# Experts in pair blocks and single blocks, value products in two halves

## The chip, the cores and the metric

The kernel runs on one core of one Trainium2 chip. The metric is the device time of one execution in microseconds; lower is better.

## The reference

A macaron layer on x of 4 x 1024 tokens with 128 features: half a mixture of experts, attention, half a mixture again, each on a layer-normed input and added to x.

```python
x = x + 0.5 * ffn(layernorm(x))
x = x + attention(layernorm(x))
x = x + 0.5 * ffn(layernorm(x))

def ffn(x):                       # D = 128, H = 512, E = 8 experts, top 2
    xf = layernorm(x, g, b)
    scores, idx = top_k(xf @ router_w, 2); gate = softmax(scores)
    # sum over the token's two experts of gate * expert(xf)
def expert(x):
    x = layernorm(x, g, b)
    x1 = x @ W1 + b1
    x2 = clip(x @ W2 + b2, -20, 20)
    hidden = clip(x1 * silu(x2), -1e4, 1e4)
    return clip(hidden @ Wo + bo, -1e4, 1e4)

def attention(x):                 # 16 heads of 8 features, q = k = v
    qkv = x @ W_qkv.T             # per head
    return (softmax(q q^T / sqrt(8)) q) @ W_o.T
```

## The kernel before, in words

There are three stages: experts, attention, experts.

**Experts.** Routing scatters every token's normed row twice into a DRAM buffer with one region per expert (`rows_dram`; a row carries its gate and where its result goes). `vector_lay_out` then computes on VectorE, from the counts of the experts, which expert and which rows each block has. A block is 256 rows (`BLOCK`), two tiles of 128, of one expert; there are 39 blocks (`BLOCKS`), enough for any split of 8192 rows over eight experts. The same program serves all counts, so unused blocks are computed too. Behind the last row of every expert stands filler, written by SyncE (`sync_experts`, L649, eight DMAs).

For a block, SyncE loads the expert's record of weights (`sync_load_record`, L687) and the rows (`sync_load_rows`, L692), six blocks ahead. TensorE turns the rows (`tensor_turn`, L1652). `tensor_chunk` (L1689, L1691) makes four chunks of the hidden layer, W2 and W1 side by side in one PSUM bank. Each f32 product is two instructions, each with its weight load, so a block has 16 of these and 8 in the second product (`tensor_second`, L1700). Per chunk VectorE clips (L1432), ScalarE applies silu (L1091) and VectorE combines (L1442). Then VectorE clips the hidden layer (L1449), TensorE makes the second product, ScalarE adds the bias (L1099), VectorE clips (L1455), TensorE turns back (L1710), ScalarE weighs by the gate tile by tile (L1108), and GpSimd scatters each tile (L963). The order on TensorE is written out in `tensor_experts`: chunk 0, turn back of block i - 2, turn of block i + 1, chunks 1 and 2, second product of block i - 1, chunk 3. Every step waits on a semaphore of the step before it.

**Attention.** The 16 heads of 4 batches are 16 teams of four heads. A team has two halves of 512 queries, and a half has 8 units (128 keys each) of four score slots, one a head. TensorE walks the slots two at a time, called a step here: `tensor_scores` (L1772 to L1778) makes two banks of scores of 128 keys by 512 queries, two row groups of the array side by side; `tensor_row_max` (L1753, L1754) makes scores the other way round into two banks, for the row maxima of a later team, which VectorE reduces (L1496, or L1501 where the two banks do not lie together). ScalarE takes the exponential of each slot (L1133). Once in two steps, `tensor_values(n)` (L1793) multiplies the four heads' exponentials of unit n by the values, 16 output columns for each head, the four heads side by side in four column groups: eight instructions of 512 columns. They add up in `value_bank` over the 8 units of a half; then ScalarE copies it (`finish`, L1151) and the half is turned, scaled and projected.

The order is fixed: at slots 4m + 2 the unit m - 1 follows.

```python
                if slot % UNIT and slot > UNIT:
                    tensor_values(slot // UNIT - 1)
```

The seven PSUM banks of attention are a ring (`Ring`, `att_bank`): whoever fills a bank waits until the seventh holder before it has been read, so a step, which takes four banks, waits for readers of the step before it and of the one before that. `tensor_values` waits until the last slot of its unit is read (`emptied(("score", UNIT * (n + 1) - 1))`), and at the first unit of a half for `value_copied`. ScalarE waits before each fourth slot for the unit two before it (`valued`), since there are eight buffers of exponentials. Chores (transposes, projections, the routing of the next stage) are planned slot by slot in `chores`. The last team has no row maxima left to make.

## Time and profile before

| what | value |
|---|---|
| median of 3 runs | 1529.58 us (1526.94 to 1529.65) |
| the profiled execution | 1530.78 us, of which 1529.0 us from its first to its last instruction |
| busy, TensorE / VectorE / ScalarE / GpSimd | 1262.8 / 1173.5 / 886.3 / 518.2 us |
| mean granted TensorE clock | 0.94 |

Times in the rows are microseconds from the start of the span unless marked ns. PE is TensorE's matmul side, PEld its weight loads, DVE VectorE, ACT ScalarE, POOL GpSimd, SPq the DMA issues of SyncE. A matmul row's time includes the end of the pipeline, so neighbours overlap; distances between starts tell the rate. Busy time of an engine is the time in which any of its instructions runs.

### The profile page before, as it was taken

How to read it: one execution, taken by the hardware profiler on the slowest of the kernel's cores; microseconds unless marked ns; L12 is line 12 of the kernel's file. 1: busy time of each engine (PE TensorE's matmuls, PEld its weight loads, DVE VectorE, ACT ScalarE, POOL GpSimd, SP SyncE). 2: the span in 40 equal slices, each digit the busy share in tenths (PEclk: the TensorE clock that was granted, in tenths of full speed). 3: DMA queues.
4: the chain of work that ended last, by engine and by line, in shares of the span. 5: the costliest groups of instructions: out<-in, count | busy, mean ns of one | idle time of the engine just before them, and what ended most of it. 6: DMA issues, size and time to landing. Idle time of an engine off the chain costs nothing.

```text
span 1529.0 us, 25190 instructions
## 1 busy us (share of the span) xinstructions
PE 1262.8 (83%) x7981; PEld 666.2 (44%) x7981; DVE 1173.5 (77%) x2246; ACT 886.3 (58%) x1874; POOL 518.2 (34%) x602
## 2 busy tenths in 40 slices
PE   2912999996269999999999999899998815999992
PEld 2911888885112222222322223222232214888882
DVE  6771888885398888888898888988989354888884
ACT  1201555553117887777778787777777703555551
POOL 2774333334512200133335324351043440333331
PEclk9999999998559999999999999999999857999996
DMA  7124455542220211102111011110100014554544
GB/s 235 37 63 160 148 187 193 191 172 84 62 81 4 81 34 33 31 12 74 33 35 48 13 54 33 33 46 18 33 2 2 29 53 157 188 195 173 188 164 167
DMA packets 66998, 135.59 MB, mean 89 GB/s; under 512 B 13660, under 2 KB 37056, under 8 KB 66580
## 3 DMA queue, kind: packets, MB, share of 16 engines
q1 hardware_dynamic: 57444, 116.45, 22.5%
q0 software_dynamic: 9088, 16.94, 3.4%
q8 instruction: 67, 1.10, 0.3%
q10 hardware_dynamic: 336, 0.59, 0.1%
q14 instruction: 63, 0.52, 0.1%
HBM read 49.21 MB, written 26.92 MB: 50 GB/s over the span
## 4 chain that ended last, share of the span: by engine, by line
PE 62%; DVE 23%; issue 5%; POOL 5%; DMA 2%; ACT 2%; SPq 2%; POOLq 0%; ACTq 0%; DVEq 0%
DVE att_neg_part L1496 13%; PE psum L1793 10%; PE psum L1700 9%; PE psum L1689 9%; PE psum L1691 9%; PE psum L1772 6%; PE psum L1753 5%; PE psum L1776 4%; POOL rows_dram L954 3%; DVE att_neg_part L1501 2%; PE psum L1635 1%; DVE stats L1228 1%; PE psum L1710 1%; PE psum L1652 1%; ACT att_probs L1133 1%
## 5 line engine op out<-in xcount | busy, mean ns | idle before, releaser
L1133 ACT ACTIVATE att_probs<-psum 128x512 f32<-128x512 f32 x1024 | 534.9, 602 | 115.3 <-PE psum L1778 82.8
L1496 DVE TENSOR_REDUCE att_neg_part<-psum 128x2 f32<-128x1024 f32 x439 | 522.3, 1221 | 96.3 <-PE psum L1754 94.8
L1793 PE MATMUL psum<-att_probs,att_values 128*16 128x512 f32 x2048 | 271.8, 603 | 0.6 <-ACT att_o_t L1151 0.3
L963 POOL DMA_INDIRECT y_dram<-ffn_y,ffn_block_rows x156 | 152.9, 980 | 336.1 <-ACT ffn_y L1108 305.0
L1091 ACT ACTIVATE ffn_silu<-ffn_x2c,ffn_rec 128x256 f32<-128x256 f32 x312 | 158.4, 508 | 158.3 <-DVE ffn_x2c L1432 158.3
L1753 PE MATMUL psum<-att_right,att_left 64*128 64x512 bf16 x512 | 198.2, 388 | 52.4 <-issue 21.8
L1432 DVE TENSOR_SCALAR ffn_x2c<-psum,ffn_rec 128x256 f32<-128x256 f32 x312 | 168.4, 540 | 92.4 <-PE psum L1691 87.6
L1775 PE MATMUL psum<-att_right,att_left 64*128 64x512 bf16 x512 | 198.3, 387 | 11.7 <-DVE att_neg_part L1496 8.8
L1772 PE MATMUL psum<-att_right,att_left 64*128 64x512 bf16 x512 | 197.7, 386 | 5.2 <-DVE att_neg_part L1496 3.7
L1754 PE MATMUL psum<-att_right,att_left 64*128 64x512 bf16 x512 | 201.1, 394 | 0.0
L1776 PE MATMUL psum<-att_right,att_left 64*128 64x512 bf16 x512 | 195.4, 382 | 0.0
L1778 PE MATMUL psum<-att_right,att_left 64*128 64x512 bf16 x512 | 194.8, 380 | 0.0
L1689 PE MATMUL psum<-ffn_block_t,ffn_rec 128*128 128x256 f32 x624 | 188.7, 384 | 1.1 <-ACT ffn_block_t L1059 1.1
L1691 PE MATMUL psum<-ffn_block_t,ffn_rec 128*128 128x256 f32 x624 | 187.5, 382 | 0.0
L1442 DVE SCALAR_TENSOR_TENSOR ffn_hidden<-psum,ffn_rec,ffn_silu 128x256 f32<-128x256 f32 x312 | 149.0, 478 | 15.8 <-ACT ffn_silu L1091 15.5
L885 POOL TENSOR_TENSOR att_max_rest<-att_max_rest,att_max_parts 16x128 f32<-16x128 f32 x64 | 27.7, 432 | 380.6 <-ACT att_max_parts L1189 378.0
L1700 PE MATMUL psum<-ffn_hidden,ffn_rec 128*128 128x256 f32 x624 | 150.1, 384 | 4.1 <-DVE ffn_hidden L1449 4.1
L954 POOL DMA_INDIRECT rows_dram<-rows,place_i x128 | 127.1, 993 | 65.9 <-issue 36.8
L1772 PEld LDWEIGHTS psum<-att_right,att_left 64*128 64x128 bf16 x512 | 47.8, 93 | 209.3 <-ACT att_probs L1133 116.8
L1700 PEld LDWEIGHTS psum<-ffn_hidden,ffn_rec 128*128 128x128 f32 x624 | 119.1, 192 | 22.1 <-DVE ffn_hidden L1449 5.8
L1691 PEld LDWEIGHTS psum<-ffn_block_t,ffn_rec 128*128 128x128 f32 x624 | 120.0, 192 | 16.8
L1753 PEld LDWEIGHTS psum<-att_right,att_left 64*128 64x128 bf16 x512 | 48.0, 94 | 175.1 <-issue 89.9
(181 smaller groups left out, 1513.5 us busy)
## 6 DMA issues: line engine op xcount, KB each, us to landing
ffn_rec<-record SPq DMA_DIRECT2D x78, 776.5 KB, 3.7
ffn_block_rows<-rows_dram SPq DMA_DIRECT2D x78, 130.0 KB, 2.1
att_left<-q_parts_dram SPq DMA_DIRECT2D x64, 96.0 KB
att_right<-q_parts_dram SPq DMA_DIRECT2D x120, 48.0 KB
record<-in_L_ffn_W SPq DMA_DIRECT2D x16, 256.0 KB, 6.7
last_y<-y_dram SPq DMA_DIRECT2D x8, 512.0 KB, 7.4
att_right<-q_parts_dram SPq DMA_DIRECT2D x90, 32.0 KB
y_dram<-ffn_y,ffn_block_rows POOLq DMA_INDIRECT x156, 2.5
```

Of the source, the lines that this page charges most:

```text
L1133: S.activation(probs[:, slot % PROBS, :], ring_bank(("score", slot))[:, :], ACT.Exp, scale=SCALE).then_inc(att_bank.by_act, 1)
L1496: last = V.tensor_reduce(out=neg_part[:, h % 2, keys, p::PAIR, t], in_=psum[:, low:high + 1, :], axis=AX.X, op=ALU.max, negate=True)
L1689: TE.matmul(both[:, 0:BLOCK], rec[:, s, W2 + c * P:W2 + (c + 1) * P], block_t[:, m % 2, :], start=True, stop=True)
L1691: TE.matmul(both[:, BLOCK:2 * BLOCK], rec[:, s, W1 + c * P:W1 + (c + 1) * P], block_t[:, m % 2, :], start=True, stop=True).then_inc(chunke ...
L1700: last = TE.matmul(y_bank[n % 2], rec[:, s, WO + c * F:WO + (c + 1) * F], hidden[:, n % 2, c, :], start=(c == 0), stop=(c == HC - 1))
L1753: TE.matmul(bank[low], left[TOP, s, p, q], right[TOP, s, p, k], start=True, stop=True)
L1754: TE.matmul(bank[high], left[BOTTOM, s, PAIR + p, q], right[BOTTOM, s, PAIR + p, k], start=True, stop=True).then_inc(maxed, 1)
L1772: TE.matmul(low, left[TOP, s, p, k], right[TOP, s, p, q], start=True, stop=False)
L1775: TE.matmul(high, left[BOTTOM, s, PAIR + p, k], right[BOTTOM, s, PAIR + p, q], start=True, stop=False)
L1776: TE.matmul(low, left[TOP, s, PAIR + p, k], right[TOP, s, PAIR + p, q], start=False, stop=True).then_inc(att_bank.filled, 1)
L1778: TE.matmul(high, left[BOTTOM, s, p, k], right[BOTTOM, s, p, q], start=False, stop=True).then_inc(att_bank.filled, 1)
L1793: last = TE.matmul(value_bank[head * VS:head * VS + VW, :], values[:, b % 2, kt, team * TEAM + head, :], probs[:, (UNIT * n + j) % PROBS, ...
```

## The change

The experts' rows are cut into tiles of 128. An expert's tiles go in pairs into blocks of two tiles (32 blocks), and those left over into blocks of one tile (8 blocks), 40 blocks in all. The pair blocks come first, the single ones last. `tiles_of` and `rows_of` give the size of a block, and loads, turns, products, clips, activations and scatters work on that many rows (`few`). `vector_lay_out` computes the owner and the first row of both kinds. A region ends with 128 rows of filler where it had 256.

In attention `tensor_values(n, part)` makes one half of the 512 queries; part 0 follows the scores and the row maximum of slot 4m, part 1 those of slot 4m + 2. Part 0 has the waits, part 1 signals `valued`.

```diff
     BLOCK = 2 * P
     BH = BLOCK // P
-    REGION = TOKENS + BLOCK
-    BLOCKS = (TOPK * TOKENS - E) // BLOCK + E
+    REGION = TOKENS + P
+    PAIRS = ((TOPK * TOKENS - E) // P + 1) // 2
+    BLOCKS = PAIRS + E
+    PAIRED, SINGLE = slice(0, PAIRS), slice(PAIRS, BLOCKS)
...
         def y_scatters(n, r):
 
-            return 16 * BH * len(range(r, n, YSETS))
+            return 16 * sum(tiles_of(m) for m in range(r, n, YSETS))
+
+        def tiles_of(n):
+
+            return BH if n % BLOCKS < PAIRS else 1
+
+        def rows_of(n):
+            return tiles_of(n) * P
...
             for e in range(E):
                 at = Q.value_load(end_i[0:1, e:e + 1], min_val=0, max_val=E * REGION)
-                Q.dma_start(rows_dram[k][bass.ds(at, BLOCK), :], filler_dram[:, :]).then_inc(filler_out[k], 16)
+                Q.dma_start(rows_dram[k][bass.ds(at, P), :], filler_dram[0:P, :]).then_inc(filler_out[k], 16)
...
             row = Q.value_load(whose_i[0:1, 1, i:i + 1], min_val=0, max_val=E * REGION)
-            Q.dma_start(block_rows[:, i % SLOTS, :, :], rows_dram[k][bass.ds(row, BLOCK), :]
-                        .rearrange("(p r) c -> p r c", r=BH)).then_inc(block_in[i % SLOTS], 16)
+            Q.dma_start(block_rows[:, i % SLOTS, 0:tiles_of(i), :], rows_dram[k][bass.ds(row, rows_of(i)), :]
+                        .rearrange("(p r) c -> p r c", r=tiles_of(i))).then_inc(block_in[i % SLOTS], 16)
...
-            settle(V.tensor_scalar(tiles_f[:, :], total, float(BLOCK - 1), None, ALU.add))
+
+            settle(V.tensor_scalar(tiles_f[:, :], total, float(P - 1), None, ALU.add))
             settle(V.tensor_copy(tiles_i[:, :], tiles_f[:, :]))
-            settle(V.tensor_scalar(tiles_i[:, :], tiles_i[:, :], BLOCK.bit_length() - 1, None, ALU.logical_shift_right))
-            settle(V.tensor_copy(tiles_f[:, :], tiles_i[:, :]))
-            settle(V.tensor_tensor_scan(tiles_end[:, :], unit[:, :], tiles_f[:, :], 0.0, ALU.mult, ALU.add))
-            settle(V.tensor_tensor(tiles_start[:, :], tiles_end[:, :], tiles_f[:, :], ALU.subtract))
-            shape = [1, BLOCKS, E]
-            blocks = block_f[:, :].unsqueeze(2).to_broadcast(shape)
+            settle(V.tensor_scalar(tiles_i[:, :], tiles_i[:, :], P.bit_length() - 1, None, ALU.logical_shift_right))
+            V.tensor_copy(tiles_f[:, :], tiles_i[:, :])
+            settle(V.tensor_scalar(pairs_i[:, :], tiles_i[:, :], 1, None, ALU.logical_shift_right))
+            settle(V.tensor_copy(pairs_f[:, :], pairs_i[:, :]))
+            started, ended = ends[:, :, 0:E], ends[:, :, 1:E + 1]
+            settle(V.tensor_tensor_scan(ended[:, 0, :], unit[:, :], pairs_f[:, :], 0.0, ALU.mult, ALU.add))
+            settle(V.tensor_scalar(ended[:, 0, :], ended[:, 0, :], float(PAIRS), None, ALU.min))
+            settle(V.tensor_tensor(in_pairs[:, :], ended[:, 0, :], started[:, 0, :], ALU.subtract))
+            V.tensor_scalar(skipped[:, 0, :], started[:, 0, :], 2.0, None, ALU.mult)
+            settle(V.scalar_tensor_tensor(singles[:, :], in_pairs[:, :], -2.0, tiles_f[:, :], ALU.mult, ALU.add))
+            settle(V.tensor_tensor_scan(ended[:, 1, :], unit[:, :], singles[:, :], 0.0, ALU.mult, ALU.add))
+            settle(V.scalar_tensor_tensor(skipped[:, 1, :], in_pairs[:, :], -2.0, started[:, 1, :], ALU.mult, ALU.add))
             V.memset(passed[:, :, 0:1], 1.0)
-            V.tensor_tensor(passed[:, :, 1:E + 1], blocks, tiles_end[:, :].unsqueeze(1).to_broadcast(shape), ALU.is_ge)
-            settle(V.tensor_tensor(within[:, :, :], blocks, tiles_start[:, :].unsqueeze(1).to_broadcast(shape),
-                                   ALU.subtract))
+            for n, some in enumerate((PAIRED, SINGLE)):
+                shape = [1, some.stop - some.start, E]
+                V.tensor_tensor(passed[:, some, 1:E + 1], block_f[:, some].unsqueeze(2).to_broadcast(shape),
+                                ended[:, n, :].unsqueeze(1).to_broadcast(shape), ALU.is_ge)
+                last = V.tensor_tensor(within[:, some, :], tile_f[:, some].unsqueeze(2).to_broadcast(shape),
+                                       skipped[:, n, :].unsqueeze(1).to_broadcast(shape), ALU.subtract)
+            settle(last)
...
             V.wait_ge(combined, HC * (m + 1))
-            V.tensor_scalar(hidden[:, m % 2, :, :], hidden[:, m % 2, :, :], LIMIT, -LIMIT,
+            few = slice(0, rows_of(i))
+            V.tensor_scalar(hidden[:, m % 2, :, few], hidden[:, m % 2, :, few], LIMIT, -LIMIT,
                             ALU.min, ALU.max).then_inc(hidden_ready, 1)
...
             both = chunk_bank[n % 4]
             if n >= 4:
                 TE.wait_ge(combined, n - 3)
-            TE.matmul(both[:, 0:BLOCK], rec[:, s, W2 + c * P:W2 + (c + 1) * P], block_t[:, m % 2, :],
+            few, w1_few = slice(0, rows_of(i)), slice(BLOCK, BLOCK + rows_of(i))
+            TE.matmul(both[:, few], rec[:, s, W2 + c * P:W2 + (c + 1) * P], block_t[:, m % 2, few],
                       start=True, stop=True)
-            TE.matmul(both[:, BLOCK:2 * BLOCK], rec[:, s, W1 + c * P:W1 + (c + 1) * P], block_t[:, m % 2, :],
+            TE.matmul(both[:, w1_few], rec[:, s, W1 + c * P:W1 + (c + 1) * P], block_t[:, m % 2, few],
...
                 for n in max_units(slot + 1):
                     tensor_row_max(n)
-                if slot % UNIT and slot > UNIT:
-                    tensor_values(slot // UNIT - 1)
+                if slot >= UNIT:
+                    tensor_values(slot // UNIT - 1, slot % UNIT // 2)
                 for chore in chores[slot] + chores[slot + 1]:
                     tensor_chore(*chore)
-            tensor_values(NSCORES // UNIT - 1)
+            for part in range(2):
+                tensor_values(NSCORES // UNIT - 1, part)
...
-        def tensor_values(n):
+        def tensor_values(n, part):
+
             i, u = divmod(n, UNITS)
             half, kt = divmod(u, BT)
             b, team = divmod(i, TEAMS)
-            TE.wait_ge(*att_bank.emptied(("prepare", b, 15)))
-            if kt == 0:
-                if 2 * i + half:
-                    TE.wait_ge(value_copied, 2 * i + half)
-                else:
-                    TE.wait_ge(value_bank_blanked, 1)
-            TE.wait_ge(*att_bank.emptied(("score", UNIT * (n + 1) - 1)))
+            if part == 0:
+                TE.wait_ge(*att_bank.emptied(("prepare", b, 15)))
+                if kt == 0:
+                    if 2 * i + half:
+                        TE.wait_ge(value_copied, 2 * i + half)
+                    else:
+                        TE.wait_ge(value_bank_blanked, 1)
+                TE.wait_ge(*att_bank.emptied(("score", UNIT * (n + 1) - 1)))
+            q = slice(part * HALF // 2, (part + 1) * HALF // 2)
             for j, head in enumerate(HEAD_OF):
-                last = TE.matmul(value_bank[head * VS:head * VS + VW, :], values[:, b % 2, kt, team * TEAM + head, :],
-                                 probs[:, (UNIT * n + j) % PROBS, :], start=(kt == 0), stop=(kt == BT - 1))
-            last.then_inc(valued, 1)
+                last = TE.matmul(value_bank[head * VS:head * VS + VW, q], values[:, b % 2, kt, team * TEAM + head, :],
+                                 probs[:, (UNIT * n + j) % PROBS, q],
+                                 start=(kt == 0 and part == 0), stop=(kt == BT - 1 and part == 1))
+            if part == 1:
+                last.then_inc(valued, 1)
```

## Rows read from the trace of the kernel before

**Rows 1.** The page, costliest groups: busy us, mean ns; idle before, releaser.

```profile
L1133 ACT ACTIVATE att_probs<-psum 128x512 f32<-128x512 f32 x1024 | 534.9, 602 | 115.3 <-PE psum L1778 82.8
L1496 DVE TENSOR_REDUCE att_neg_part<-psum 128x2 f32<-128x1024 f32 x439 | 522.3, 1221 | 96.3 <-PE psum L1754 94.8
...
L1091 ACT ACTIVATE ffn_silu<-ffn_x2c,ffn_rec 128x256 f32<-128x256 f32 x312 | 158.4, 508 | 158.3 <-DVE ffn_x2c L1432 158.3
...
L1432 DVE TENSOR_SCALAR ffn_x2c<-psum,ffn_rec 128x256 f32<-128x256 f32 x312 | 168.4, 540 | 92.4 <-PE psum L1691 87.6
...
L1442 DVE SCALAR_TENSOR_TENSOR ffn_hidden<-psum,ffn_rec,ffn_silu 128x256 f32<-128x256 f32 x312 | 149.0, 478 | 15.8 <-ACT ffn_silu L1091 15.5
```

**Rows 2.** Stretches: length, busy PE, PEld, DVE, ACT, POOL, clock, DMA share, GB/s.

```profile
160.01:362.08 202.07, 202.07 (x1008) 177.84 (x1007) 166.83 (x360) 118.34 (x287) 70.77 (x72) 1.00 0.48 174
...
455.71:1176.90 721.19, 685.94 (x5161) 202.59 (x5164) 629.69 (x866) 562.24 (x1124) 212.77 (x289) 1.00 0.12 33
1176.90:1223.01 46.11, 38.38 (x274) 11.06 (x273) 19.16 (x69) 33.36 (x69) 18.92 (x22) 0.89 0.08 25
```

**Rows 3.** Timeline of TensorE over one block of experts: start, duration, line.

```profile
255.37 1.89 PE L1700 MATMUL psum<-ffn_hidden,ffn_rec 128*128 128x256 f32 x8
...
260.99 0.38 PE L1700 MATMUL psum<-ffn_hidden,ffn_rec 128*128 128x256 f32 x1
```

**Rows 4.** Timeline of TensorE over one round of attention.

```profile
803.39 0.39 PE L1772 MATMUL psum<-att_right,att_left 64*128 64x512 bf16 x1
...
803.83 0.38 PE L1753 MATMUL psum<-att_right,att_left 64*128 64x512 bf16 x1
...
804.26 0.38 PE L1776 MATMUL psum<-att_right,att_left 64*128 64x512 bf16 x1
...
804.77 0.37 PE L1753 MATMUL psum<-att_right,att_left 64*128 64x512 bf16 x1
...
805.09 1.05 PE L1793 MATMUL psum<-att_probs,att_values 128*16 128x512 f32 x8
806.07 0.39 PE L1772 MATMUL psum<-att_right,att_left 64*128 64x512 bf16 x1
```

**Rows 5.** Timeline of ScalarE and VectorE in the same round.

```profile
804.02 2.07 ACT L1133 ACTIVATE att_probs<-psum 128x512 f32<-128x512 f32 x4 [0.62 <-PE psum L1778]
...
804.25 2.36 DVE L1496 TENSOR_REDUCE att_neg_part<-psum 128x2 f32<-128x1024 f32 x2 [0.33 <-PE psum L1754]
```

**Rows 6.** Timeline of TensorE, a projection of 128 columns in attention.

```profile
626.15 1.16 PE L1827 MATMUL psum<-wo_t,att_xh_t 128*128 128x128 f32 x8
```

**Rows 7.** Chain that ended last, first stage: the fold, one column wide.

```profile
59.03 3.20 PE psum L1601 x16
```

**Rows 8.** Groups by line, VectorE from SBUF to SBUF: busy us, mean ns.

```profile
L1449 DVE TENSOR_SCALAR ffn_hidden<-ffn_hidden 128x1024 f32<-128x1024 f32 x78 | 54.1, 694 | 2.7
...
L1455 DVE TENSOR_SCALAR ffn_y_t<-ffn_y_t 128x256 f32<-128x256 f32 x78 | 23.3, 299 | 35.3 <-ACT ffn_y_t L1099 35.3
```

**Rows 9.** Timeline of the tail of the first experts' stage.

```profile
367.23 3.18 PE L1700 MATMUL psum<-ffn_hidden,ffn_rec 128*128 128x256 f32 x8 [1.80 <-DVE ffn_hidden L1449]
...
372.02 0.62 ACT L1108 ACTIVATE ffn_y<-psum,ffn_block_rows 128x128 f32<-128x128 f32 x2 [1.11 <-PE psum L1710]
373.42 0.98 POOL L963 DMA_INDIRECT y_dram<-ffn_y,ffn_block_rows  x1 [3.94 <-ACT ffn_y L1108]
374.71 0.98 POOL L963 DMA_INDIRECT y_dram<-ffn_y,ffn_block_rows  x1 [0.30 <-issue]
```

**Rows 10.** Timeline before the second experts' stage: SyncE's fillers, the layout's end.

```profile
1251.28 9.73 SPq L649 DMA_DIRECT2D rows_dram<-filler_dram  x8
...
1254.92 0.39 DVE L1394 CAST whose_i<-whose 1x78 int32<-1x78 f32 x1
```

**Rows 11.** Timeline of ScalarE, the copy of the value bank.

```profile
616.06 0.59 ACT L1151 COPY att_o_t<-psum 128x512 f32<-128x512 f32 x1
```

**Rows 12.** Timeline of TensorE, the last team.

```profile
1188.55 1.05 PE L1793 MATMUL psum<-att_probs,att_values 128*16 128x512 f32 x8
...
1190.50 1.05 PE L1793 MATMUL psum<-att_probs,att_values 128*16 128x512 f32 x8
```

54 lines of the change are left out of this document (35 added, 19 removed).

## Prediction

> **What bounds the kernel now.** I read the page first. Its costliest groups [rows 1] belong to two different stages, the exponentials and row maxima of attention and the clips and products of the experts, on all three engines; so the next view is the table of stretches [rows 2]. In the first experts' stage TensorE is busy for the whole 202.07 us, VectorE for 166.83: TensorE sets the pace, and whatever shortens its work shortens the stage. In attention (721.19 us for 15 of the 16 teams) TensorE is busy 685.94, VectorE 629.69 and ScalarE 562.24, but that busy time includes the overlapping ends of matmuls; only the order of starts tells what is work and what is wait.
>
> The timeline of a block of experts [rows 3] shows the eight second products starting at 255.37 and again at 260.99: 5.62 us for one block. Eight products of 256 columns take 1.89, so (1.89 - 0.38) / 7 = 0.216 each, the last one lasting 0.38; 24 products at 0.216 are 5.18, and the four transposes get the other 0.44, 0.11 each. 36 blocks lie in the 202.07 us, 5.61 each.
>
> The timeline of attention [rows 4] shows one round of four score slots, one unit of value products: scores at 803.39, a row maximum at 803.83, the second scores, whose last products start at 804.26, the row maximum at 804.77, values at 805.09, the next scores at 806.07: 2.68 us. Scores cost 0.44, and a row maximum 0.22. The second row maximum would follow 804.26 by 0.22 and starts 0.29 after that: it needs the bank of the score whose exponential starts at 804.02 [rows 5], lasts 0.60 [rows 1] and is seen by TensorE at 804.77, a release of 0.15. This is the one wait in an ordinary round. VectorE's two maxima take 2.36 of the 2.68 and ScalarE's four exponentials 2.07 [rows 5]. So the round is TensorE's work, 2.39, plus 0.29 of waiting. The 240 units of 15 teams are 643 us at that rate; the other 78 are chores (transposes, projections, routing) and VectorE's busier rounds.
>
> **The change part by part: experts.** Each stage has 39 blocks of two tiles now, 32 of two and 8 of one after: 7 blocks of 5.62 go (39.3 us), 8 small ones come. A small block issues the same 24 products with the same weights on 128 columns, and two transposes. Half of 0.216 would be 0.108. The nearest row for 128 columns and 128x128 f32 weights is the projection of attention [rows 6]: eight in 1.16, or 0.126 each if the last one lasts about as long as a transpose, 0.28. The bound on the other side is the fold of the first stage, one column wide [rows 7]: 16 in 3.20, 0.20 each, where nothing covers the weight load. I take 0.126, since width and weights agree: 24 x 0.126 + 2 x 0.11 + 0.06 = 3.3 us. By 0.20 it would be 5.1, by 0.108 2.9.
>
> The Trainium skill ("TensorE: Matmul & The Clock Gate", LDWEIGHTS) says that a weight load costs its columns divided by 1.2 GHz; for 128 that is an estimate of 107 ns, which would make a small block about 2.9 us. The trace's 0.126 is above it.
>
> VectorE and latency must fit into the 3.3. Durations by width, from SBUF: 694 against 299 ns for 1024 and 256 elements, 0.51 ns each [rows 8]; from PSUM (1221 - 540) / 768 = 0.89 ns each, maxima against clips [rows 1]. So a clip goes from 540 to about 430 ns, a combine from 478 to 365, a silu from 508 to about 400, the clip of hidden from 694 to 430, that of y from 299 to 230. VectorE's ten add up to 3.8; neighbours overlap, as the maxima do by 0.08 (two in 2.36 at 1.22 each), which brings it to 3.1: just inside. Latency is the tighter one: the second product of a block waits for the last clip (0.43), silu (0.40), combine (0.37), clip of hidden (0.43) and four hand-overs, about 1.9 us after the last first product; TensorE has three chunks and two transposes, 1.7, to put there. I add 0.2: 3.5 us a small block, bounds 2.9 and 5.1. Per stage: -39.3 + 28.0 = -11.3.
>
> The small blocks stand last, so the tail behind the last block shortens too. Its eight second products take 3.18 us [rows 9], 0.4 each where a full block has 0.216; by the 0.126 doubled they would be 2.1, and I take 0.9 off. One transpose of two saves 0.2, the vector and scalar steps about 0.8, one weighing of two 0.3 (two take 0.62, [rows 9]), and one scatter of two 1.29, the distance of their issues. That is -3.5 a stage. Both stages: 2 x (-11.3 - 3.5) = -30.
>
> **The layout** of blocks gets some eight more VectorE instructions of 0.16 to 0.2 us. In the second stage they run under the eight fillers of SyncE, which take 9.73 us [rows 10], and the layout before ends 1255.31, 5.7 before those do; cost nothing, 1.5 without that cover. The fillers move half as many bytes: between 0 and -2, I take -1.
>
> **Attention.** A unit's eight value products of 512 columns become twice eight of 256, one half after every row maximum. A unit costs 0.98 from its start to the next scores: two waves of 2 x 0.216, and 0.12 more. And the step into it costs 0.32 after a row maximum, where the next scores would come after 0.22: 0.10 more. These two extras, 0.22, are paid twice per round. A half is 0.43 + 0.12 = 0.55. A step is then 0.22 + 0.22 + 0.32 + 0.55 = 1.31 to 1.32, a round 2.63. Does the wait come back? The row maximum needs the previous step's first exponential, seen at 0.63 + 0.60 + 0.15 = 1.38 after its scores; it now comes at 1.31 + 0.44 = 1.75. The wait of 0.29 is gone. But the first half of a unit now follows the scores of slot 4m and needs the exponential of slot 4m - 1, where before it had a step more. That is seen at 0.63 + 0.49 + 0.60 + 0.15 = 1.87, the values stand at 1.31 + 0.76 = 2.07: 0.2 to spare. VectorE needs 2.36 of 2.63. So 2.68 becomes 2.63, -0.05 a round; rounds in which VectorE sets the pace gain nothing, I count 180 of 240: -9.
>
> The Trainium skill ("TensorEngine Tiling (Array Packing)", Key Properties) says that a change of tiling mode drains the engine. The trace agrees with its 0.10 before and 0.12 behind a unit; the rule speaks against halves.
>
> Two places lose. At the end of each half of a team the value bank is copied (0.59, [rows 11]), and the next unit, which waits for the copy, now starts a step earlier. The copy stands behind two exponentials, starts 0.63 + 2 x 0.49 = 1.61 after the scores and is seen at 2.35, against 2.07: 0.28 x 30 = +8. Behind the copying ScalarE instruction stand the next exponentials, 0.15 late, which is within their slack. And the last team has rounds without row maxima, 1.95 apart [rows 12]. Apart from the unit's 0.98 a round there is 0.44 and 0.22 of scores and 0.31 of step into the unit. A step would be 0.22 + 0.31 + 0.55 = 1.08, with the first half waiting for 1.87 instead of 1.08 + 0.53: 2 x 1.08 + 0.26 = 2.42, +0.47 over 11 rounds: +5. Attention: -9 + 8 + 5 = +4.
>
> **Sum:** -30 - 1 + 4 = -27. The profiled execution took 1530.8 (1529.0 of span, 1.8 around it), 1.2 over the median of 1529.6; a difference carries over unchanged: 1529.6 - 27 = 1502.6, say 1503.
>
> **The rivals.** (A, forecast, 0.62.) Experts give 30, attention about nothing. Own range 1490 to 1515, from small blocks of 2.9 to 4.1 us and 0.05 us either way a round.
>
> (B, 0.10.) Halves are really half: 0.49 instead of 0.55, no extra switches, a step 1.25 and a round 2.50. 0.18 x 240 = 43 instead of 9: 1469. For it speaks that VectorE would still fit (2.36); against it that no value group in the trace is followed by scores in under 0.98.
>
> (C, 0.12.) Small blocks are bound by weight loads at 0.20, or by the latency chain at 5.1 us: a stage changes by 8 x 5.1 - 39.3 = +1.5, less 3.5 of tail, both -4; with -1 and +4 the total is -1: 1529. At 4.3 us it would be 1516. The 0.126 speaks against it.
>
> (D, other side, 0.16.) The first half of a value unit waits for the exponential in most rounds, because ScalarE falls behind by more than the 0.2 it has. With the exponential seen 0.45 later than I reckon, every first half is 0.24 late and a round is 2.87: 0.24 x 240 = +58, 1561. It decides from 0.11 a round upward, where it eats the 27. For it: ScalarE's copies of 0.59 stand in the same queue; against it: it has 0.27 idle a step to catch up.
>
> **The numbers.** Slower comes from most of D (0.11; its mild part lands below). No measurable change is 0.2%, 3 us, on either side: half of C and the edge of D, 0.07. The rest, 0.82, is faster. The range runs from between A and B to C: 1484 to 1530, which leaves B and most of D out.
>
> **What would show it.** Experts: second products of the last 7 blocks 3.3 to 3.7 apart, 5.62 in the others; the stage ends some 14 us sooner. In attention, value groups 1.31 apart with row maxima directly behind score pairs; PE should show short waits for ScalarE's o_t copy; the last team's rounds near 2.4. Wrong would be: small blocks at 5 us, value halves preceded by a ScalarE wait everywhere, or a value half taking 0.49.

## The result and the profile after

The changed kernel takes 1502.11 us (median of 4 runs, 1501.35 to 1503.41), the kernel before 1528.26 beside it (4 runs, 1525.86 to 1529.65): a ratio of 0.9833, 95% interval 0.9817 to 0.9849, or 26.2 us less. The forecast was 1503. The profiled span fell from 1529.0 to 1500.9, by 28.1.

First the page of the changed kernel, the groups that answer to [rows 1]. The exponentials are as many and about as long as before; the 4,096 value products are now 256 wide. The clips and silus of the experts are 320 instead of 312, shorter in the mean.

```profile
L1156 ACT ACTIVATE att_probs<-psum 128x512 f32<-128x512 f32 x1024 | 556.6, 596 | 120.4 <-PE psum L1821 90.5
L1536 DVE TENSOR_REDUCE att_neg_part<-psum 128x2 f32<-128x1024 f32 x439 | 530.0, 1223 | 76.7 <-PE psum L1797 63.3
L1839 PE MATMUL psum<-att_probs,att_values 128*16 128x256 f32 x4096 | 320.9, 385 | 6.8 <-ACT att_o_t L1174 4.2
...
L1113 ACT ACTIVATE ffn_silu<-ffn_x2c,ffn_rec 128x256 f32<-128x256 f32 (+1 forms) x320 | 154.8, 487 | 152.2 <-DVE ffn_x2c L1469 152.2
L1469 DVE TENSOR_SCALAR ffn_x2c<-psum,ffn_rec 128x256 f32<-128x256 f32 (+1 forms) x320 | 163.2, 513 | 90.3 <-PE psum L1732 86.4
```

Then the table of stretches, with the columns of [rows 2]. The marks are the same events in both kernels: from the first to the last group of second products of an experts' stage, and from the first value group of a team to that of another.

```profile
160.25:362.40 202.15, 194.25 (x1035) 172.04 (x1033) 163.85 (x379) 116.66 (x294) 68.80 (x70) 0.99 0.47 176
444.70:1158.30 713.60, 701.08 (x7077) 210.30 (x7076) 641.44 (x862) 578.56 (x1124) 213.05 (x289) 1.00 0.12 34
1158.30:1208.30 50.00, 41.19 (x397) 12.51 (x397) 20.39 (x76) 36.48 (x71) 18.92 (x22) 0.93 0.07 23
1271.90:1475.80 203.90, 198.88 (x1061) 175.60 (x1061) 168.49 (x389) 119.61 (x302) 68.44 (x70) 1.00 0.47 174
```

Laid beside [rows 2] this gives the account of the whole span. Fifteen teams: 721.2 to 713.6, -7.6. The last team: 46.1 to 50.0, +3.9. The first experts' stage, from the first group of second products (154.1 before, 154.5 after) to the last (367.2 and 362.4): 213.1 to 207.9, -5.2; the second 213.1 to 203.9, -9.2. Behind the first stage, up to the first value group, -6.2, of it 1.5 because the first half of a unit comes one step of slots earlier (it starts 5.6 behind attention's first scores, the whole unit of before 7.1); behind the second, to the end, 28.8 to 25.1, -3.7. Between attention and the second stage -0.5, and the first stage begins 0.4 later. The sum is -28.1.

Now TensorE over the experts' blocks of one tile. The first row of each block is its transpose of the input (L1692, where an idle time is shown), then its eight second products (L1742).

```profile
332.71 1.16 PE L1742 MATMUL psum<-ffn_hidden,ffn_rec 128*128 128x128 f32 x8 [0.16 <-DVE ffn_hidden L1488]
...
336.19 1.16 PE L1742 MATMUL psum<-ffn_hidden,ffn_rec 128*128 128x128 f32 x8 [0.19 <-DVE ffn_hidden L1488]
...
340.22 0.33 PE L1692 MATMUL psum<-identity,ffn_block_rows 128*128 128x128 f32 x1 [1.82 <-DMA ffn_rec<-record]
341.28 1.06 PE L1742 MATMUL psum<-ffn_hidden,ffn_rec 128*128 128x128 f32 x8
...
345.87 0.33 PE L1692 MATMUL psum<-identity,ffn_block_rows 128*128 128x128 f32 x1 [2.48 <-DMA ffn_rec<-record]
347.68 1.91 PE L1742 MATMUL psum<-ffn_hidden,ffn_rec 128*128 128x128 f32 x8
```

From 332.71 to 336.19 are 3.48 us: the small block of the forecast, 3.5. The next two are 5.09 and 6.40 apart. TensorE stood still for 1.82 and 2.48 us before their transposes, for the load of the expert's weights. Right behind the second idle time the granted clock fell to half, 1.2 GHz, for 3.4 us from 346.1; the products at 347.68 lie in it and take 1.91 instead of 1.16. The record of weights that the second idle time waits for was issued at 342.17 (first fence) and needs 3.6 us to land. The table of waits of SyncE's queue, from 320 to 364, says why it was issued so late (second fence): before it issues a block's loads (L709) SyncE waits for the scatter of the block six before.

```profile
342.17 0.50 SPq L705 DMA_DIRECT2D ffn_rec<-record  x1
```

```profile
SPq L709 <- DMA y_dram<-ffn_y,ffn_block_rows: 13.8, 5, 5.3
```

The DMA engines were not full meanwhile. In the table of stretches their share from 340 to 343, just before the second idle time, is 0.11 (last but one column):

```profile
340.00:343.00 3.00, 2.78 (x25) 2.78 (x25) 1.75 (x7) 1.62 (x5) 0.65 (x1) 1.00 0.11 22
```

Last, TensorE in attention, one ordinary round and the end of a half team, with row maxima (L1796) and value halves (L1839). Value groups stand 1.31 apart, a round is 2.62. At 560.12 the copy of the value bank holds the first half up by 0.17. The last team, without row maxima, has one such wait for an exponential in each round (second fence), 2.43 long where it was 1.95 [rows 12].

```profile
555.64 0.38 PE L1796 MATMUL psum<-att_right,att_left 64*128 64x512 bf16 x1
...
555.95 0.63 PE L1839 MATMUL psum<-att_probs,att_values 128*16 128x256 f32 x8
556.51 0.39 PE L1815 MATMUL psum<-att_right,att_left 64*128 64x512 bf16 x1
...
557.26 0.62 PE L1839 MATMUL psum<-att_probs,att_values 128*16 128x256 f32 x8
...
558.57 0.62 PE L1839 MATMUL psum<-att_probs,att_values 128*16 128x256 f32 x8
...
560.12 0.62 PE L1839 MATMUL psum<-att_probs,att_values 128*16 128x256 f32 x8 [0.17 <-ACT att_o_t L1174]
```

```profile
1172.28 0.63 PE L1839 MATMUL psum<-att_probs,att_values 128*16 128x256 f32 x8 [0.17 <-ACT att_probs L1156]
...
1173.38 0.62 PE L1839 MATMUL psum<-att_probs,att_values 128*16 128x256 f32 x8
...
1174.71 0.63 PE L1839 MATMUL psum<-att_probs,att_values 128*16 128x256 f32 x8 [0.17 <-ACT att_probs L1156]
```

### The profile page after: what moved, and what is told of

It reads as the page before. It is cut to its first block, busy times and chain, and to the rows that moved or that the text cites. A ratio compares the mean times of both kernels' runs of the same rounds, so it can differ in the third digit from the quotient of the medians.

```text
span 1500.9 us, 29407 instructions
## 1 busy us (share of the span) xinstructions
PE 1252.9 (83%) x10053; PEld 656.3 (44%) x10053; DVE 1173.0 (78%) x2286; ACT 895.3 (60%) x1874; POOL 506.2 (34%) x593
## 3 DMA queue, kind: packets, MB, share of 16 engines
q1 hardware_dynamic: 58020, 116.18, 22.8%
## 4 chain that ended last, share of the span: by engine, by line
PE 46%; DVE 18%; issue 4%; ACT 3%; DMA 2%; SPq 2%; POOL 1%; DVEq 0%; POOLq 0%; ACTq 0%
PE psum L1839 13%; DVE att_neg_part L1536 10%; PE psum L1815 7%; PE psum L1819 5%; PE psum L1796 4%; PE psum L1730 4%; PE psum L1732 4%; PE psum L1742 4%; DVE att_neg_part L1541 1%; ACT att_probs L1156 1%; DVE stats L1253 1%; ACT att_o_t L1174 1%; PE psum L1862 1%; DVE x_sb L1505 1%; PE psum L1890 1%
## 5 line engine op out<-in xcount | busy, mean ns | idle before, releaser
L1156 ACT ACTIVATE att_probs<-psum 128x512 f32<-128x512 f32 x1024 | 556.6, 596 | 120.4 <-PE psum L1821 90.5
L1536 DVE TENSOR_REDUCE att_neg_part<-psum 128x2 f32<-128x1024 f32 x439 | 530.0, 1223 | 76.7 <-PE psum L1797 63.3
L1839 PE MATMUL psum<-att_probs,att_values 128*16 128x256 f32 x4096 | 320.9, 385 | 6.8 <-ACT att_o_t L1174 4.2
L984 POOL DMA_INDIRECT y_dram<-ffn_y,ffn_block_rows x144 | 141.2, 980 | 326.5 <-ACT ffn_y L1131 301.7
L1113 ACT ACTIVATE ffn_silu<-ffn_x2c,ffn_rec 128x256 f32<-128x256 f32 (+1 forms) x320 | 154.8, 487 | 152.2 <-DVE ffn_x2c L1469 152.2
L1469 DVE TENSOR_SCALAR ffn_x2c<-psum,ffn_rec 128x256 f32<-128x256 f32 (+1 forms) x320 | 163.2, 513 | 90.3 <-PE psum L1732 86.4
L1796 PE MATMUL psum<-att_right,att_left 64*128 64x512 bf16 x512 | 198.3, 388 | 33.0 <-issue 21.4
L1730 PE MATMUL psum<-ffn_block_t,ffn_rec 128*128 128x256 f32 (+1 forms) x640 | 181.3, 365 | 1.1 <-ACT ffn_block_t L1080 1.1
L1732 PE MATMUL psum<-ffn_block_t,ffn_rec 128*128 128x256 f32 (+1 forms) x640 | 180.5, 364 | 0.0
L1839 PEld LDWEIGHTS psum<-att_probs,att_values 128*16 128x16 f32 x4096 | 68.0, 94 | 223.5 <-issue 124.7
L1480 DVE SCALAR_TENSOR_TENSOR ffn_hidden<-psum,ffn_rec,ffn_silu 128x256 f32<-128x256 f32 (+1 forms) x320 | 144.5, 451 | 18.4 <-ACT ffn_silu L1113 16.9
L1742 PE MATMUL psum<-ffn_hidden,ffn_rec 128*128 128x256 f32 (+1 forms) x640 | 140.4, 363 | 6.4 <-DVE ffn_hidden L1488 6.4
L1815 PEld LDWEIGHTS psum<-att_right,att_left 64*128 64x128 bf16 x512 | 47.4, 93 | 198.1 <-ACT att_probs L1156 127.2
L1742 PEld LDWEIGHTS psum<-ffn_hidden,ffn_rec 128*128 128x128 f32 x640 | 113.2, 192 | 22.7 <-DVE ffn_hidden L1488 9.5
```

The source lines that it names most:

```text
L1156: S.activation(probs[:, slot % PROBS, :], ring_bank(("score", slot))[:, :], ACT.Exp, scale=SCALE).then_inc(att_bank.by_act, 1)
L1536: last = V.tensor_reduce(out=neg_part[:, h % 2, keys, p::PAIR, t], in_=psum[:, low:high + 1, :], axis=AX.X, op=ALU.max, negate=True)
L1730: TE.matmul(both[:, few], rec[:, s, W2 + c * P:W2 + (c + 1) * P], block_t[:, m % 2, few], start=True, stop=True)
L1732: TE.matmul(both[:, w1_few], rec[:, s, W1 + c * P:W1 + (c + 1) * P], block_t[:, m % 2, few], start=True, stop=True).then_inc(chunked, 1)
L1742: last = TE.matmul(y_bank[n % 2][:, few], rec[:, s, WO + c * F:WO + (c + 1) * F], hidden[:, n % 2, c, few], start=(c == 0), stop=(c == HC ...
L1796: TE.matmul(bank[low], left[TOP, s, p, q], right[TOP, s, p, k], start=True, stop=True)
```

## Experiments

They ran in three groups, each on one chip and against the kernel before on the same chip: e1 to e4 (before 1577.86, 18 runs), e5 to e8 (1582.92, 9 runs), e9 to e12 (1579.12, 9 runs). All kernels are some 50 us longer there than in the result above, so only ratios are compared across groups; e12 looks at those 50 us.

### e1: the experts' part alone

The changed kernel with value products whole, as before.

```diff
-                if slot >= UNIT:
-                    tensor_values(slot // UNIT - 1, slot % UNIT // 2)
+                if slot % UNIT and slot > UNIT:
+                    tensor_values(slot // UNIT - 1)
...
```

> The experts' half of the change alone: 32 pair blocks and 8 single ones, value products whole as before. By the prediction's sum the experts give 30 and the fillers 1: 1497. By the reading of the changed kernel's trace, where the second products of the last blocks are 3.48 us apart but two or three gaps in each stage are 4.2 to 6.4, a stage gives 5 to 9 and its tail 3.7: together 22 to 24 off, 1505. Under 1500 the first holds, over 1503 the second.

Measured: 1558.24, ratio 0.9873 (0.9858 to 0.9888), 20.0 us less (17.7 to 22.4). The gain of the change is in the experts, but it is smaller than the 31 of the forecast's terms for them, and near the 22 to 24 read from the trace.

### e2: the value halves alone

The kernel before with the halves, the same lines the other way round.

> The attention's half of the change alone: 39 blocks of two tiles, value products in two halves after every row maximum. The prediction's sum gives +4 (rounds of 2.63 for 2.68, +0.28 at each copy of the value bank, +0.47 a round in the last team): 1532. The trace of the changed kernel suggests about 8 off in 15 teams and 4 on in the last: 1525. Rival: the halves are worth nothing by themselves and the whole gain is the experts': 1529, rounds of 2.68.

Measured: 1579.71, ratio 1.0008 (0.9999 to 1.0017): +1.3 us. The time is the rival's, but not for its reason: the rounds of the third team are 2.62 and not 2.68, and it is the last team and the stalls (e12) that take the gain back. The sum of e1 and e2 is -18.7 here; the whole change on the next chip (e5) gives -21.

### e3: both halves one behind the other

The kernel before, both halves issued at the place of the whole unit.

```diff
                 if slot % UNIT and slot > UNIT:
-                    tensor_values(slot // UNIT - 1)
+                    for part in range(2):
+                        tensor_values(slot // UNIT - 1, part)
...
```

> The kernel before with both halves of a unit of value products issued one behind the other where the whole unit stood (slots 4m + 2). If the price of a half is its place between products of another shape (0.22 us for each entry and exit), the unit costs 0.98 as before and the time stays at 1529, rounds of 2.68. If halving itself costs (twice as many instructions and weight loads, 0.03 to 0.1 a unit), the rounds get longer by that and 240 of them add 7 to 24 us.

Measured: 1582.01, ratio 1.0029 (1.0018 to 1.0039), +4.5 us. The rounds of the trace are 2.69, those of before, and beside e12 each team without a stall but the first is the same to 0.1 us, some 1 us together. A group of sixteen starts 0.990 ahead of the next scores (median), the whole unit of eight 0.985. So twice as many products of half the width cost next to nothing where no other shape stands between them. What halves cost in the change is the second entry and exit, as the forecast had it. Of the 4.5 us some 2 lie in longer stalls (e12); the rest was not located.

### e4: one more buffer for the blocks' loads

The changed kernel with seven sets of input buffers for blocks instead of six, so that SyncE waits for the scatter of the block seven before.

```diff
-    SLOTS = 6
+    SLOTS = 7
```

> The changed kernel with seven instead of six buffers of records and rows, so that a block's load is issued one block sooner. If the gaps of 4.2 to 6.4 us between single blocks come from loads that are issued too late, behind the scatter of the block six before, they shrink to 3.5 and the time falls by 3 to 8 us: 1496. If they come from the DMA engines being full (a record of 776 KB in 3.5 us is 222 GB/s), they stay or move and the time stays within 2 us, or the seventh record before the second stage costs 1.6 more.

Measured: 1553.53, ratio 0.9849 (0.9835 to 0.9862). TensorE's timeline has small blocks 3.48 to 3.55 apart but for one of 3.9 in each stage, whose turn back waits for VectorE, and the stages take 203.0 and 203.1 instead of 207.9 and 203.9:

```profile
353.02 0.39 PE L1732 MATMUL psum<-ffn_block_t,ffn_rec 128*128 128x128 f32 x2
353.67 1.16 PE L1742 MATMUL psum<-ffn_hidden,ffn_rec 128*128 128x128 f32 x8 [0.27 <-DVE ffn_hidden L1488]
...
357.15 1.16 PE L1742 MATMUL psum<-ffn_hidden,ffn_rec 128*128 128x128 f32 x8 [0.27 <-DVE ffn_hidden L1488]
```

SyncE's waits for scatters have not gone; in the same stretch they have grown from 13.8 to 18.6 us:

```profile
SPq L709 <- DMA y_dram<-ffn_y,ffn_block_rows: 18.6, 5, 5.3
```

But no transpose waits for a load any more. The wait of a queue costs nothing until an engine with work stands behind it, and one more buffer puts it out of reach. DMA engines too slow for a record in 3.48 us, the expectation's other branch, would have kept the gaps: that is out.

The traces of all kernels say it more broadly. Eight stages with six buffers (the result, e1, e5, e6) take 203.9 to 208.1, eight with seven (e4, e8, e9, e10) 202.9 to 203.4. What late loads cost thus varies from one execution to the next, 1 to 5 us a stage. In the time of the whole kernel the gain is 4 us where the halves are absent (e1 against e10, in different groups); with them the intervals of e4 and e5 overlap.

### e5: the changed kernel again

No edit, the partner of e6 on its chip.

> The changed kernel once more, beside the others of this group: it gives the profile and the time on the same chip. 26 us under the kernel before if the chips agree. On the chip of the first group the runs had three stalls of 14 to 16 us in attention that neither first trace has, in teams 7, 11 and 15; if they belong to the chip, they are here or not here in all four kernels; if they belong to a kernel, only in some.

Measured: 1561.95, ratio 0.9863 (0.9848 to 0.9878), against 0.9833 in the result: 21 us less and not 26. The stalls (e12) are in all four kernels of this group.

### e6: whole units where a half has to wait

The changed kernel, both halves together at the later place in the units behind a copy of the value bank and in those behind the last row maximum.

```diff
-                if slot >= UNIT:
-                    tensor_values(slot // UNIT - 1, slot % UNIT // 2)
+                unit = slot // UNIT - 1
+                if slot >= UNIT and (unit % BT == 0 or not max_units(slot + 1)):
+                    if slot % UNIT:
+                        tensor_values(unit, 0)
+                        tensor_values(unit, 1)
+                elif slot >= UNIT:
+                    tensor_values(unit, slot % UNIT // 2)
```

> The changed kernel, but the first unit of each half of a team and the units behind the last row maximum are made whole at slots 4m + 2 as before. If the first half waits for the copy of the value bank and, in the last team, for the exponential, as the prediction has it, the rounds of 2.86 become 2.69 (30 x 0.17 = 5) and those of 2.43 become 1.95 (11 x 0.47 = 5): 10 us under the changed kernel. Rival: the 0.24 is ScalarE's delay and comes back a round later, then 5 or less.

Measured: 1558.93, ratio 0.9853 (0.9833 to 0.9873), which the interval doesn't part from e5. The traces do. The last team has rounds of 1.95 again and takes 62.9 instead of 68.0, each with a stall in it (e12). At the copies nothing came: the group of 16 behind the copy stands a step later, and the next one is nearer by as much.

```profile
517.93 0.62 PE L1844 MATMUL psum<-att_probs,att_values 128*16 128x256 f32 x8
520.35 1.06 PE L1844 MATMUL psum<-att_probs,att_values 128*16 128x256 f32 x16
522.67 0.62 PE L1844 MATMUL psum<-att_probs,att_values 128*16 128x256 f32 x8
```

In units, measured between their first products, the two rounds around the copy are 3.73 and 2.33 here and 2.86 and 3.20 in e5, 6.06 in both, and the second and third teams take 45.1 and 43.9 here and 45.1 and 44.0 there. So the rival was right at the copies: the delay comes back a moment later. That it is ScalarE's queue which would charge it is the likely reason and was not tested alone.

### e7: values ahead of the row maximum

A theory of mine: with whole products, placed before the row maximum, TensorE would fill the time in which it waits for the bank. The kernel before with two lines exchanged:

```diff
-                for n in max_units(slot + 1):
-                    tensor_row_max(n)
                 if slot % UNIT and slot > UNIT:
                     tensor_values(slot // UNIT - 1)
+                for n in max_units(slot + 1):
+                    tensor_row_max(n)
```

> The kernel before with one edit: at slots 4m + 2 the whole unit of value products stands ahead of the row maximum instead of behind it. If a round is 2.39 of TensorE's work and 0.29 of waiting for the exponential before the second row maximum, a whole unit (0.98) covers this wait as halves do, without a second entry and exit: rounds of 2.39 to 2.42, VectorE (2.36) just behind. 0.27 x 150 to 200 rounds: 40 to 54 off. Rival: the second row maximum now comes 0.98 later, VectorE idles meanwhile and the wait moves to it: rounds of 2.6 to 2.7, gain under 15.

Measured: 1660.43, ratio 1.049 (1.0476 to 1.0504), +78 us. Every ordinary round is 3.23 long. The timeline of one round, TensorE (scores L1772 and L1775, row maximum L1753) and VectorE:

```profile
559.51 1.05 PE L1793 MATMUL psum<-att_probs,att_values 128*16 128x512 f32 x8
...
560.50 0.39 PE L1753 MATMUL psum<-att_right,att_left 64*128 64x512 bf16 x1
...
560.93 2.36 DVE L1496 TENSOR_REDUCE att_neg_part<-psum 128x2 f32<-128x1024 f32 x2 [0.88 <-PE psum L1754]
...
562.21 0.39 PE L1775 MATMUL psum<-att_right,att_left 64*128 64x512 bf16 x1 [0.47 <-DVE att_neg_part L1496]
...
562.74 1.05 PE L1793 MATMUL psum<-att_probs,att_values 128*16 128x512 f32 x8
```

The value group delays the row maximum by 0.98, VectorE idles 0.88 for it, its reduction ends later, and the next scores (L1775) wait 0.47 for the bank that it holds; they in turn delay the next value group. TensorE and VectorE each wait once a round. The order that fills TensorE's wait starves VectorE, whose two maxima need 2.36 of the 2.68 us. The theory is wrong; the rival had the mechanism but not its size (rounds of 2.6 to 2.7).

### e8: the same order with the experts' part and seven buffers

> The experts' half of the change, seven buffers, and whole units of value products ahead of the row maximum. If the three effects add up: 20 (experts), 4 to 6 (seventh buffer), 40 to 54 (order): 64 to 80 under the kernel before. If the order is worth under 15, 25 to 41.

Measured: 1635.25, ratio 1.032 (1.0304 to 1.0335), rounds of 3.23 again. It was meant as the best version, and falls with e7; from e7 to e8 the experts' part and the seventh buffer take 25 us off.

### e9: seven buffers, and whole units only behind the last row maximum

The changed kernel with the edit of e4 and that part of e6 that brought something.

```diff
-    SLOTS = 6
+    SLOTS = 7
...
+                if slot >= UNIT and not max_units(slot + 1):
+                    if slot % UNIT:
+                        tensor_values(unit, 0)
+                        tensor_values(unit, 1)
+                elif slot >= UNIT:
+                    tensor_values(unit, slot % UNIT // 2)
```

> The changed kernel with seven buffers, and with whole units of value products behind the last row maximum only (the part of the mended kernel that shortened a stretch: the last team took 5 less, the copies nothing). The changed kernel stood at 0.986 on the slower chip and 0.983 on the first. 5 off for the last team and 4 to 6 for the single blocks: 10 under the changed kernel, a ratio of 0.979 to 0.980 on the slower chip. If the two do not add up, 0.983.

Measured: 1550.19, ratio 0.9824 (0.9809 to 0.9840), the fastest version of the study, by its interval below e1 and e5, while those of e4, e6 and e10 overlap it. The 0.979 to 0.980 was missed: the two terms did not add up, and against e5's ratio it is 6 us and not 10.

### e10: the experts' part with seven buffers

> The experts' half of the change with seven buffers, attention wholly as before. The experts' half alone gave 0.987; 4 to 6 for the seventh buffer: 0.984. It is the version to prefer if the halves are worth nothing; against the kernel of the same group with halves it shows what halves are worth once the last team is spared: by the traces 45 of 48 us come in teams 0 to 14 at 0.5 a team less, 7 off. So it should be 0.5% slower than that one, or the same if the longer stalls of the slower chip eat it.

Measured: 1555.31, ratio 0.9846 (0.9832 to 0.9859), 0.0027 or 4 us below e1's ratio, with intervals that just touch. The two experts' stages take 203.2 and 203.0 in its trace, 207.5 and 205.0 in e1's. Against e9, on the same chip, it isolates the halves where row maxima are: e9's trace has fifteen teams in 745.7 us, e10's in 749.6, -3.9; thirteen teams give -5.3 of it, the two with a stall +1.3. That is less than the 7 expected.

### e11: the clip of hidden cut to a quarter in small blocks

The kernel of e4; in the small blocks the clip leaves out three of the four chunks of hidden.

```diff
-            V.tensor_scalar(hidden[:, m % 2, :, few], hidden[:, m % 2, :, few], LIMIT, -LIMIT,
+            chunks = slice(0, HC) if rows_of(i) == BLOCK else slice(HC - 1, HC)
+            V.tensor_scalar(hidden[:, m % 2, chunks, few], hidden[:, m % 2, chunks, few], LIMIT, -LIMIT,
```

> The changed kernel with seven buffers, whose single blocks clip only the last of the four chunks of the hidden layer (the clip of the other three is left out). If a single block's 3.48 us are TensorE's work plus the wait of the second product for this clip (0.43, would be 0.23), the single blocks come 3.28 to 3.32 apart. If weight loads or VectorE's own load set the 3.48, the distance stays.

Measured once: 1552.07. The small blocks come 3.28 apart instead of 3.48, and the rows of the second products show no idle time any more:

```profile
348.07 1.16 PE L1743 MATMUL psum<-ffn_hidden,ffn_rec 128*128 128x128 f32 x8
...
350.96 0.39 PE L1733 MATMUL psum<-ffn_block_t,ffn_rec 128*128 128x128 f32 x2
351.34 1.16 PE L1743 MATMUL psum<-ffn_hidden,ffn_rec 128*128 128x128 f32 x8
...
354.62 1.16 PE L1743 MATMUL psum<-ffn_hidden,ffn_rec 128*128 128x128 f32 x8
```

It looks as if 3.28 were TensorE's own work in a small block, but it is not, for these rows include the end of the pipeline. The distances of starts tell more: the pairs of first products stand 0.22 to 0.23 apart, and from the last pair, 350.96, to the second products are 0.38, so 0.16 of waiting is left. The table of waits of the weight loads, from 343 to 361, has it:

```profile
PEld psum L1743 <- DVE ffn_hidden L1489: 1.2, 5, 0.3
```

Another 0.06 stands before the turn back. In e4 the last pair starts at 353.02 and the second products at 353.67, 0.65 later: a wait of 0.43, of which the row shows 0.27. Both kernels give the same work, 3.48 - 0.43 and 3.28 - 0.16 - 0.06, or 3.05 to 3.06. What sets the distance is the chain from the last first products of a block through clip, silu, combine and clip of hidden to its second products, since it got shorter by just the 0.2 of the edit. VectorE's own load is not wholly out as a rival, for the edit takes 0.2 off that too. It is busy 9.42 of 10.45 us over three blocks of e4, so it is close behind.

### e12: the kernel before, with a profile on this chip

> The kernel before, for its profile on this chip. If the three stalls of 14 to 16 us belong to the chip and not to an edit, teams 7, 11 and 15 have them here too, each about 15 long, and everything else in the trace agrees with the first one within 1 us a team.

Measured once: 1576.31, span 1574.6. The extra time sits in three places: teams 7 and 11 take 63.5 and 63.8 us (48.0 and 48.1 in the profile of the kernel before above) and the last 58.7 (46.1). In each, GpSimd makes a run of 16 routing scatters. TensorE and the chain that ended last, in one of them:

```profile
818.69 0.55 PE L1776 MATMUL psum<-att_right,att_left 64*128 64x512 bf16 x1
819.02 0.63 PE L1778 MATMUL psum<-att_right,att_left 64*128 64x512 bf16 x1
827.29 0.58 PE L1753 MATMUL psum<-att_right,att_left 64*128 64x512 bf16 x1 [7.63 <-ACT att_probs L1133]
```

```profile
813.48 1.75 another core or an unknown queue
...
817.95 7.14 another core or an unknown queue
825.13 1.43 another core or an unknown queue
```

The kernel before, the experts alone (63.3 and 63.7) and the changed kernel (63.7 and 64.5) all have them, at the same two teams. They belong to the chips or the time of these groups and not to the change. In kernels with the halves they are longer: the last team takes 58.7 to 61.6 with whole units (e12, e1, e10) and 65.4 to 68.0 with halves there (e4, e2, e5), of which the longer rounds explain some 4 to 5. One thing in this trace is not as in the first: the last of the fifteen teams, without a stall in either, takes 50.5 here and 51.7 there. With whole units e1 and e10 have 50.6.

## Why the forecast was right, and which of its terms were not

**Bound and mechanism.** Forecast A came in: experts give nearly all. Attention gives 5 in the result's pair of traces and nothing in e2. B is out, since halves are 1.31 apart and not 1.25. C's 5.1 us a small block is out, by 3.48. D is out: of 240 first halves in fifteen teams 21 waited for the copy, 0.2 at most, and none for an exponential by the table of waits of the matmuls. The weight loads have 138 such waits, but they are hidden: first and second halves both start 0.30 to 0.31 behind the row maximum (555.64 and 555.95 above).

**A small block: the sum right, its two parts not.** 3.48 against 3.5. TensorE's own work was forecast as 3.3 and is 3.05. The second products take 1.16 for eight, as the row chosen [rows 6], 0.124 apart. But the sixteen first products stand only 0.111 apart (a pair every 0.22, e4), where all 24 were priced at 0.126. The wait for the second product was forecast as 0.2 and is 0.43: the chain behind the last first product takes 2.04 and not 1.9 (351.63 to 353.67 in e4), and TensorE has 1.61 of work to put there, not 1.7. That the two errors cancel is luck; the latency chain as the tighter bound, which the forecast named, is confirmed by e11. The durations by width, in the changed kernel's single blocks:

```profile
L1469 DVE TENSOR_SCALAR ffn_x2c<-psum,ffn_rec 128x128 f32<-128x128 f32 x29 | 11.4, 406 | 4.1 <-PE psum L1732 4.1
L1113 ACT ACTIVATE ffn_silu<-ffn_x2c,ffn_rec 128x128 f32<-128x128 f32 x29 | 11.4, 401 | 9.6 <-DVE ffn_x2c L1469 9.6
L1480 DVE SCALAR_TENSOR_TENSOR ffn_hidden<-psum,ffn_rec,ffn_silu 128x128 f32<-128x128 f32 x29 | 10.1, 347 | 2.7 <-ACT ffn_silu L1113 2.1
...
L1488 DVE TENSOR_SCALAR ffn_hidden<-ffn_hidden 128x512 f32<-128x512 f32 x8 | 3.4, 427 | 0.3
```

That is 406, 401, 347 and 427 ns where the forecast had 430, 400, 365 and 430.

**A stage: the term that was mis-sized.** "Per stage: -39.3 + 28.0 = -11.3" measured -5.2 and -9.2; the term was 8.2 us too large over both. It multiplied the small block by eight and asked only whether TensorE, VectorE and the latency fit into it. Two things were left out. The loads have to keep up as well: SyncE's chain of scatter, landing and load goes round once in six blocks, and six small blocks are 21 us where six large ones were 34. That cost 4.9 us in the first stage, the half clock behind the second idle time included, and 0.8 in the second (207.9 and 203.9 against 203.0 and 203.1 with the seventh buffer, e4). And with seven buffers a stage gives -10.1, 1.2 short of the term, because the blocks beside the small ones are not as reckoned. The step from large to small goes over 5.51, 5.18 and 4.49 where 5.62, 5.62 and 3.5 were counted (0.4), one small block takes 3.9 (0.4), and the last two distances of the kernel before were already 5.40 and 5.31 instead of 5.62 (0.5).

**The tail: too small, by the clock.** "That is -3.5 a stage" measured -3.7, and -4.7 in the first (the 6.2 less the 1.5 of the halves). From the last second products to the last scatter's issue it was 367.23 to 374.71 [rows 9], 7.48; in the changed kernel:

```profile
362.36 1.16 PE L1742 MATMUL psum<-ffn_hidden,ffn_rec 128*128 128x128 f32 x8 [1.27 <-DVE ffn_hidden L1488]
...
365.75 0.98 POOL L984 DMA_INDIRECT y_dram<-ffn_y,ffn_block_rows  x1 [2.28 <-ACT ffn_y L1131]
```

or 3.39. The products took 2.0 off and not 0.9, but the smaller block did only 0.8 of it. In the kernel before the granted clock fell to half at 367.9, while they ran, and in the changed kernel at 366.6, behind the tail. In e2, which has the experts of before, it stayed full until 380.1: there the eight take 1.99, and the last scatter is issued 6.05 behind their start. Against that the 3.39 is 2.7 less; the other 1.4 is the clock. The forecast saw that the 3.18 is twice the usual spacing and carried that over to the small block, where it did not occur. Both stages with their tails: -22.8 for -30. The layout and fillers are -0.5 before the second stage and +0.4 before the first, for the -1. Together it is -22.9 by this trace, -20.0 by e1's ratio.

**Attention: the round right, the sum wrong.** A round is 2.62 for 2.63, the copy adds 0.24 for 0.28, the last team's round is 2.43 for 2.42 and the last team +3.9 for +5, since seven of its rounds are 2.43 and not eleven. Yet the total is not +4: -7.6 in fifteen teams, -1.5 at the start and +3.9 are -5.2. The rounds of a half team, taken from the third team's trace, were 3.27, 2.81, 2.90 and five of 2.69, and are 3.20, 2.62, 2.82, four of 2.62 and the copy's 2.86: 0.45 less. The forecast had six at -0.05 and one +0.28, nearly nothing. It missed 0.02 in each round (2.69 to 2.62 where it had 2.68 to 2.63), and the second round behind a copy, which loses 0.19. In the kernel before, that round (553.65 to 556.46 in the third team) has a wait for VectorE that no ordinary round has, as the table of waits of TensorE's weight loads from 553.6 to 556.6 shows:

```profile
PEld psum L1775 <- DVE att_neg_part L1496: 0.5, 1, 0.5
```

The halves leave it out. Teams in which VectorE sets the pace gain nothing, as forecast (50.6 to 50.5), so the mean is 0.25 a half team; times 30, that is the -7.6, where the forecast's -9 and +8 left -1. Not all of the -7.6 is the halves': 1.2 of it come from the last of the fifteen teams, 51.7 in this one trace of the kernel before and 50.5 in e12, so some 6.4 are theirs.

**Two errors that cancelled.** The forecast had 8 us too much gain from the experts and 9 too little from attention: -28.1 in the trace against its -27. The median fell 26.2. The sum hit by luck better than its terms deserve.

**Where the experiments ran** the halves are worth nothing or less (e2, +1.3), and the change 21 instead of 26. Thirteen of fifteen teams still gain 5.3 (e9 against e10); the stalls of e12, longer with halves, and the last team's slower rounds eat it.

## What to carry to other kernels

When blocks get smaller, ask of every ring of buffers what it holds in time, not only in blocks: the same six buffers held 34 us of work and then 21, and what had been hidden came out on TensorE; one more buffer gave most of it back. A round repeated 200 times has to be read from several of its neighbours, the odd ones behind a copy too, to the hundredth of a microsecond. The idle time that a matmul row shows is less than the wait, by the end of the pipeline in the row before; only distances of starts, set against a place without a wait, give the work of a block. And an instruction moved ahead to fill a gap of one engine (e7) is to be priced by what it delays on the engine that is nearly as busy.

## What the runs showed of the hardware

**Halving products.** Eight value products of 512 columns and sixteen of 256 issued together both take 1.05 us (1.05 in e7, 1.06 in e6); a group of eight halves between other shapes starts 0.56 ahead of the next scores (557.26 to 557.82), and twice that is 1.12 for the 0.98 of a whole unit [rows 4].

**Scatters among the small blocks land no later.** The table of DMA issues has the scatters from 330 to 355, among the small blocks, landing a median of 2.9 us after their issue (first fence). Among the large blocks, from 250 to 275, it is 3.0 (second fence), and 2.5 over all scatters of either kernel.

```profile
y_dram<-ffn_y,ffn_block_rows POOLq DMA_INDIRECT x7, 2.9
```

```profile
y_dram<-ffn_y,ffn_block_rows POOLq DMA_INDIRECT x10, 3.0
```

Single ones take more than 5 us in both kernels (5.2 in the changed one, 5.4 in the kernel before, both issued near 308). What changed is the time that the ring leaves them, and not the landing. What makes single ones late was not tested.

**Stalls of all engines.** In all three groups of runs PE, ACT and DVE stood for up to 8.6 us at a time within a stretch of some 15 us, three times a run, each time while GpSimd issued its 16 routing scatters, one every 1.26 us. The same scatters in the profile of the result's kernels passed with no stall. The profile names "another core or an unknown queue" as the releaser, and in e12 the granted clock is at half, 1.2 GHz, from 818.8 to 832.4, once TensorE has begun to stand. What holds the engines stays open: no run here varied the scatters.
